# The first expert matmul in two halves of 64 output rows, in a block of its own

## What is computed

```python
probs = jax.nn.softmax(x2 @ wr, axis=-1)
gate_v, gate_i = jax.lax.top_k(probs, TOP_K)
...
buf = jnp.zeros((E, C, H), x2.dtype).at[ef, posc].add(tok)
h = jax.nn.gelu(jnp.einsum('ech,ehf->ecf', buf, w1) + b1[:, None, :])
y = jnp.einsum('ecf,efh->ech', h, w2) + b2[:, None, :]
ys = y[ef, posc] * (gf * keep)[:, None]
moe_out = ys.reshape(T, TOP_K, H).sum(axis=1).reshape(B, S, H)
return x + moe_out
```

## Time and profile before

| | us |
|---|---|
| median of 3 runs | 422.57 |
| lowest and highest run | 422.13 and 425.06 |
| span of the profiled execution, first to last instruction | 420.9 |
| its PE busy time | 329.6 |
| its ACT, DVE and POOL busy time | 223.2, 233.6, 200.1 |
| mean granted TensorE clock | 0.844 |

### The profile page before, as it was taken

One profiled execution on the slowest core, in us unless ns is written; L12 is line 12 of the kernel. 1 busy time (PEld: TensorE's weight loads), 2 busy tenths in 40 slices (PEclk: granted clock), 3 DMA queues, 4 the chain that ended last, 5 costly groups with the idle time before them and its releaser, 6 DMA issues.

```text
span 420.9 us, 10393 instructions
## 1 busy us (share of the span) xinstructions
PE 329.6 (78%) x3936; PEld 283.9 (67%) x3936; DVE 233.6 (56%) x615; ACT 223.2 (53%) x640; POOL 200.1 (48%) x312
## 2 busy tenths in 40 slices
PE   8858767888859558876978666369999899999960
PEld 6646556776546446654767545259999899999950
DVE  1475886744397967887558675453333333333324
ACT  2346657776686645585476743300454555555530
POOL 3177586568640131622214656562255455555550
PEclk9998999999688765596689856557999999999995
DMA  8999903000000000000000000004789898999406
GB/s 280 374 404 258 116 21 96 2 2 1 2 2 2 2 2 2 0 4 0 3 2 2 11 19 18 6 11 116 205 310 301 282 319 318 321 314 316 142 12 168
DMA packets 21235, 50.14 MB, mean 119 GB/s; under 512 B 4116, under 2 KB 10340, under 8 KB 21058
## 3 DMA queue, kind: packets, MB, share of 16 engines
q1 hardware_dynamic: 18146, 46.96, 35.3%
q0 software_dynamic: 3040, 2.52, 2.2%
HBM read 43.97 MB, written 7.72 MB: 123 GB/s over the span
## 4 chain that ended last, share of the span: by engine, by line
PE 56%; DVE 16%; ACT 11%; POOL 6%; issue 5%; DMA 3%; SPq 1%; another core or an unknown queue 0%; POOLq 0%; DVEq 0%
PE bank L762 35%; PE scores L762 17%; ACT work L1063 5%; DVE mx L1292 3%; DVE work L1301 2%; DVE stats L1229 2%; POOL rstd L647 2%; DMA work<-in_patches 2%; ACT norm L1063 2%; PE bank L771 1%; PE bank L837 1%; ACT src L1063 1%; ACT xT L1063 1%; PE bank L1005 1%; DVE sm L1310 1%
## 5 line engine op out<-in xcount | busy, mean ns | idle before, releaser
L1063 ACT ACTIVATE work<-scores,b1T 128x72 f32<-128x72 f32 x256 | 61.2, 322 | 69.9 <-PE scores L762 65.9
L762 PE MATMUL bank<-ring,work 128*72 128x128 f32 x512 | 97.2, 274 | 0.0
L762 PE MATMUL scores<-work,ring 128*128 128x72 f32 x512 | 89.1, 258 | 1.3 <-DVE work L1435 1.1
L754 POOL DMA_INDIRECT expert_rows<-work,put_u x64 | 59.8, 935 | 63.0 <-issue 43.6
L762 PEld LDWEIGHTS scores<-work,ring 128*128 128x128 f32 x512 | 76.9, 191 | 1.7 <-DVE work L1435 1.2
L1063 ACT ACTIVATE work<-bank 128x288 f32<-128x288 f32 (+2 forms) x136 | 47.4, 375 | 52.4 <-PE bank L762 35.0
L1461 DVE TENSOR_SCALAR work<-bank,work 72x128 f32<-72x128 f32 x64 | 22.2, 347 | 70.5 <-issue 46.8
L762 PEld LDWEIGHTS bank<-ring,work 128*72 128x72 f32 x512 | 53.8, 145 | 0.2 <-ACT work L1063 0.2
L645 POOL TENSOR_SCALAR rstd<-mv 96x3 f32<-96x3 f32 x32 | 9.5, 296 | 71.2 <-DVE mv L1232 70.1
L762 PE MATMUL bank<-xTp,wT 128*128 128x288 f32 x80 | 36.6, 614 | 4.5 <-ACT xTp L1063 2.6
L762 PE MATMUL bank<-wT,xTp 128*128 128x128 f32 x192 | 29.4, 317 | 2.7 <-ACT work L1063 2.7
(11 more groups left out here) (157 smaller groups left out, 611.5 us busy)
## 6 DMA issues: line engine op xcount, KB each, us to landing
ring<-in_experts SPq DMA_DIRECT2D x64, 512.0 KB
work<-in_patches SPq DMA_DIRECT2D x3, 864.0 KB, 10.9
slot_rows<-hid SPq DMA_DIRECT2D x1, 2340.0 KB, 30.7
work<-slot_rows SPq DMA_DIRECT2D x7, 292.5 KB
wT<-in_weights SPq DMA_DIRECT2D x1, 1664.0 KB, 14.5
expert_rows<-mid POOLq DMA_DIRECT2D x2, 576.0 KB, 5.1
ring<-expert_rows SPq DMA_DIRECT2D x4, 288.0 KB, 4.3
expert_rows<-work,put_u POOLq DMA_INDIRECT x64
```

The lines of the kernel that those rows point to most:

```text
L754: pool.indirect_dma_start(out=ytok[:, :], out_offset=bass.IndirectOffsetOnAxis(ap=put_u[:, e:e + 1], axis=0), in_=ys[0:CAP, e % NY, :], in ...
L762: return nc.tensor.matmul(o, a, b, start=start, stop=stop)
L1063: return nc.scalar.activation(o, i, f, **kw)
```

## The change

The constant PART = 64 is new. In a step with e < E the first matmul is written in a block of its own ahead of the loop over c. In it every chunk c is computed in two parts of 64 output rows: the stationary operand has 64 columns of the weights, and the result goes to partitions 0 to 63 or 64 to 127 of the same 72 columns of scores. The second matmul keeps its loop and its instructions. SP's wait ahead of a ring transfer looks at y_full, which the second matmul's last instruction counts, in place of ys_ready.

```diff
+PART = 64
...
             for e in range(RING, E):
                 s = e % RING
-                sp.wait_ge(S["ys_ready"], e - RING + 1)
+                sp.wait_ge(S["y_full"], e - RING + 1)
                 sp.dma_start(ring[:, s, :], ins["experts"][e]).then_inc(w_here[s], 16)
...
+                if e < E:
+                    for c in range(FC):
+                        for u in range(0, D, PART):
+                            last = mm(scores[u:u + PART, e % 3, CAP * c:CAP * c + CAP], ring[:, e % RING, D * c + u:D * c + u + PART],
+                                      xe[:, e % NX, :])
+                    last.then_inc(S["h_in"], 1)
                 for c in range(FC):
-                    if e < E:
-                        last = mm(scores[:, e % 3, CAP * c:CAP * c + CAP], ring[:, e % RING, D * c:D * c + D], xe[:, e % NX, :])
-                        if c == FC - 1:
-                            last.then_inc(S["h_in"], 1)
                     if f >= 0:
                         last = mm(banks[f % 2][0:CAP, 0:D], hT[:, f % NX, c, :], ring[:, f % RING, FF + D * c:FF + D * c + D],
                                   start=(c == 0), stop=(c == FC - 1))
```

## The result

The changed kernel is slower: 434.74 us in the median (433.3 to 437.37, 4 runs) against 423.26 for the kernel before (422.13 to 425.06, 4 runs), a ratio of 1.0285 (95% interval 1.0234 to 1.0336). I had forecast 427.9, +5.3, with a range of 422 to 437.5 for the time; the measured difference is +11.5, more than twice the forecast. The direction holds, the size doesn't.

The account below looks back on a forecast made before the run. PE was taken to bound the expert stage at 1.70 us a step. A step of 1.79 gave +5.6 us over 62 steps, less 0.25 at the end: +5.3 on 422.57, so 427.9 us, range 422 to 437.5.

Parts of the forecast that it names:

- The step's price: Expert stage: a step grows from 1.70 to 1.79 us, over 62 steps +5.6 us; bounds +1.9 to +14.9.
- step (5): SP's earlier ring loads hide nothing: 0; one place where VectorE is late may go or come twice, ±1.3 us.
- the slow first block: Rival: halves side by side but as slow as the attention's scores, 0.67 for 0.52; step 1.94, 437.2 us; chance 0.08.
- step (1): First matmul's halves run side by side, 8 rounds at 0.065; 0.52 us from first to last start, bounds 0.455 and 0.67.
- The attention's scores: Existing eight-tile matmuls, eight rounds of the same width in 64 records, taken as the halves' upper bound: 0.67 us.
- step (2): Two tile-shape changes a step: next load and matmul start only 0.07 before the previous end; each costs 0.16 us.
- step (3): Second matmul runs by itself, eight records in a row: 0.84 us first to last start, then 0.11 to the transpose.
- step (4): Waits stay ahead of both blocks and what they look at comes no later; the stage's end gains 0.25 us.
- Shape changes for nothing: Rival: shape changes cost nothing inside the expert loop; step 1.48, −13.6 us, 409 us; chance 0.10.
- Halves one after the other: Rival: first-matmul halves run serially, 16 × 0.065; 440 us without shape changes paid (chance 0.05), 460 us with them (0.04).
- Loads not hidden in column tiles: Rival: halves' weight loads don't overlap as both tiles use the same rows; block 0.96, step 2.23, 455 us; chance 0.03.

Follow-up runs that it names:

- e6: Changed kernel with both halves written to partitions 0 to 63, one array tile, upper half of the result left out: 453.56 us, ratio 1.0863.
- e7: Changed kernel with the halves back in the loop over c, in turn with the second matmul, eight shape changes a step: 476.96 us, ratio 1.1423.
- e2: Kernel before with only SP's wait changed from ys_ready to y_full: 417.82 us, ratio 1.0009.
- e10: Changed kernel unmodified, run a third time, in a series with late counts: 433.61 us, ratio 1.0274.
- e11: Changed kernel with SP's wait back at ys_ready, in a series with late counts: 433.96 us, ratio 1.0263.
- e5: Changed kernel unmodified, run again; no late counts in the profiled execution: 421.9 us against 417.67 for the kernel before, ratio 1.0103.
- e1: Changed kernel with SP's wait back at ys_ready, in a series without late counts: 419.76 us against 418.25 for the kernel before, ratio 1.004.
- e9: Kernel before, unchanged, profiled in a series with late counts: 423.38 us, ratio 1.0021.
- e13: Changed kernel without SP's 53 ring transfers (experts from 11 on use weights already in the slots), in a series with late counts: 436.83 us, ratio 1.0327.
- e16: Changed kernel unmodified, run to show the kind of its series, which had late counts: 437.36 us, ratio 1.0339.
- e15: Halves with two experts to a step, rerun in a series with late counts: 436.8 us against 423.25 for the kernel before, ratio 1.0325.
- e14: Changed kernel with the halves in turn with the second matmul, rerun in a series with late counts: 481.05 us, ratio 1.1372.
- e12: Two experts to a step but whole first matmuls (PART = 128), against the kernel before, in a series with late counts: 432.08 us, ratio 1.0236.
- e4: Changed kernel without SP's 53 ring transfers, in a series without late counts: 420.3 us, ratio 1.0041.

## Why the prediction was right in its direction and wrong in its size

The step's price was mis-sized (+5.6 us for a measured +2.4), and the larger miss goes the other way: the sum lets each of the 62 steps last as long as an undisturbed one and has, for counts that come late, nothing but the ±1.3 us of step (5). In the first series the late counts cost 7.7 us: 9.5 between the two profiles from the first transpose to the last matmul, less the 1.9 that stay where nothing is late. That the measured 434.74 still lies inside my range is luck: its upper end was priced by the slow first block, which didn't happen.

**The first block, step (1).** That the halves run side by side was right (e6). I took 0.52 from first to last start; 0.72 less one record of 0.226 is 0.49. The attention's scores, my upper bound of 0.67, were no guide.

**The changes of shape, step (2).** Right: 0.07 before the end at both places, 0.16 and 0.15 us. The page of the Trainium skill that I had cited (TensorEngine Tiling (Array Packing), Key Properties) says that changing the mode drains the engine, and e7, with eight changes in a step, agrees: 0.15 us for each.

**The second block, step (3).** I had 0.84 from first to last start and it is 1.09 − 0.27 = 0.82, with 0.11 to the transpose as foreseen. The three small excesses, rounding among them, make the 0.05 between my 1.79 and the 1.74: the term was +5.6 us and measured +2.4.

**The waits, step (4).** Their order was read rightly, and in an undisturbed series none of them costs anything. What failed is "what they look at comes no later": it takes for granted that PE's counts reach the others at once, however many instructions a step has. A step has eight more matmuls and eight more loads now (38 records to 54), and the only rates that I had looked at were bursts (64 records in 0.56 us). In the disturbed series the kernels that would run 14.3 and 15.4 matmuls a us come down to some 13 over tens of us, PE's counts come 1 to 2.6 us late, and 7 to 11 us go. The one place of the earlier trace rows was the sign of it in the profile of before. I put ±1.3 us on it and called its cause a late VectorE, but there ACT and DVE too took up work together, at 326.87 and 326.93, for counts that were due at 325.1 and 325.3.

**SP's wait, step (5).** Worth 0, as said (e2, and e10 against e11).

**The rivals.** Shape changes for nothing: out, by e7. Halves one after the other: out, by e6. Loads not hidden in column tiles (TensorE: Matmul & The Clock Gate, The mechanism, in the Trainium skill: a load overlaps running matmuls only where the row group differs): out, and the trace doesn't agree with the page, since a round takes 0.062 us with loads of 64 columns in it for both tiles, as little as a record of 72 columns took before (0.065), while both tiles use all 128 rows. The slow first block, whose 437 us lay nearest the measured 434.7, would have come to it by the wrong mechanism.

In the undisturbed series the changed kernel stood at 1.0103 in e5 and its twin at 1.004 in e1: between +1.5 and +4.2 us, with my +5.3 just above. Their profiles are alike (112.15 us from the first transpose to the last matmul in both), so what parts the two ratios isn't known. In the first series it was +11.5: 2.4 from the step, some 6 from longer steps in the stage (7.8 against 1.8), and 1.5 behind the last transpose, where late counts go on (8.3 us to the last matmul against 6.7); small gains at the head and tail take 0.4 off, and the two profiles differ by 9.5 from the first transpose to the last matmul. Another 1.7 of their difference lie ahead of the stage (first transpose at 296.35 against 294.66) and are scatter: in e10 and e9 it is 2.0 the other way.

**What stays open.** What the resource behind the late counts is. It doesn't go with the ring's traffic (e13), nor with the line of the wait (e11). More matmuls a us bring more of it (e16 and e15 against the kernel before and e14), but e12 shows that the rate isn't the only condition. Both a supply of instructions that can't keep up and the writing of the records from which profiles are made would fit, and every timed run here was itself recorded, so no run tells them apart.

The kept traces lean to the second. The transfers of instructions are no slower where counts come late: in 300 to 400 us the queue that moves them in pieces of 16 KB shows 13 pieces in e5, of 0.9 to 1.4 us each, and 11 in e16, of 0.9 to 1.5. The records themselves are what differs. In the first 290 us, ahead of the stage, all these kernels do the same. There the engines' semaphore updates leave 1782 or 1783 records in every trace of the undisturbed series and 1519 to 1554 in every trace of the disturbed ones, while PE's own records differ by less than 2%. In the whole trace the kernel before has 3520 and 3544 of them (first series and e9), while e2, the same kernel but for SP's wait, has 4760 in an undisturbed series. So in the disturbed series records are lost, in the kernel before too. In e14's stage (305 to 390 us) there are 1220, against 1228 in e7, the same kernel in an undisturbed series, and there nothing is late. That the writing of records holds up PE, and that part of the +11.5 us is therefore made by the measurement, is not shown; an execution without a profile would decide it.

Nor is it known why some series have it and others don't. It isn't the chip by itself: e1 to e4 and e13 to e16 ran on the same one. The disturbed series are slower ahead of the stage too, whatever the kernel: the first transpose starts at 294.5 to 297.8 us there and at 291.1 to 293.3 in the others.

## What to carry to other kernels

Price a split matmul by three things: its streaming rounds, the changes of tile shape per step (0.15 us each here), and the loads that no longer hide. Do the tiled part for two experts at once, and the changes halve. Then ask what the instruction rate will be over tens of microseconds, not in a burst: here a kernel at 10 matmuls with their loads per us lost 1.3 us to late counts in its stage (7 to 20 us for those at 14 and more), and in other series none of them lost anything. A gain that was measured in one series (0.984 for the pairs) was a loss of 3% in another, so measure such a change more than once, and without the profiler where that can be done. A long step in the old profile in which several engines resume at the same instant is the sign to look for, and semaphore records that are missing from the trace are another.

## What the runs showed of the hardware that I had not expected

Two column tiles of 64 with 72 moving columns, both over all 128 rows, take 0.062 us a round with their loads, and 0.49 us for sixteen records; in one tile the same sixteen take 0.99 from first to last start (1.21 less 0.226).

Late counts: in three series out of five, all consumers of PE's counts resumed together, 1 to 2.7 us late (up to 3.7 in e15), while PE went on with what it had for up to 1 us and then stood. In windows of 60 us PE's throughput was 12.6 to 13.1 matmuls a us there, each with its load, for kernels that run 14.3 and 15.4 otherwise. At 9.5 a us (e14) there was none, at 10.1 (before) one long step early in the stage, at 9.1 (e12) three late counts. Whether an execution that isn't recorded has them is not known.
